# Two overlapped batches: a loop of passes with barriers, or one sequence of 256 head slots

## The reference

```
x = x + tanh(g_xattn[0]) * L0_xattn(layernorm(x), ctx)   # CoPE attention
x = x + tanh(g_ffn[0])   * L0_ffn(layernorm(x))          # 8 experts (top 2) and a shared one
x = x + tanh(g_xattn[1]) * L1_xattn(layernorm(x), ctx)   # plain cross attention
x = x + tanh(g_ffn[1])   * L1_ffn(layernorm(x))          # self attention, gated by head
```

```
pos = minimum(flip(cumsum(flip(sigmoid(logits)))), 63)
cope = logits_int[ceil(pos)] * w + logits_int[floor(pos)] * (1 - w),  w = pos - floor(pos)
scores = softmax(logits + cope);  out = scores @ V
```

## Time and profile before

| | |
|---|---|
| median of three runs | 5707.96 us |
| profiled execution, its own time | 5699.91 us |
| span of that execution | 5698.2 us |
| instructions | 64460 |
| VectorE, TensorE, ScalarE, GpSimd busy | 73%, 59%, 40%, 25% |
| bytes moved | 41.52 MB |

### The profile page before, as it was taken

How to read it: one execution, slowest core, us unless ns; L and a number is a source line. 1 busy time by engine, 2 the same in 40 slices (tenths; PEclk the granted TensorE clock), 3 DMA queues, 4 the chain that set the end, 5 groups by cost and what they waited for, 6 DMA issues and landing times. The chain is left out here.

```text
span 5698.2 us, 64460 instructions
## 1 busy us (share of the span) xinstructions
PE 3375.8 (59%) x21126; PEld 2228.9 (39%) x21126; DVE 4138.4 (73%) x8874; ACT 2277.8 (40%) x5185; POOL 1398.0 (25%) x1125
## 2 busy tenths in 40 slices
PE   3256575655657566565665656556575665756576
PEld 2133352433435334352443534334352443524353
DVE  3878597685967858588585967859588585977853
ACT  2434344343434434344343443434344343443432
POOL 0322223131222312223131321312223131231310
PEclk7567686777768677686776867667786776868776
DMA  3000000000000000000000000000000000000000
GB/s 115 0 8 1 10 1 1 10 1 10 1 8 3 1 10 1 10 1 1 10 1 10 1 1 10 1 10 1 10 1 1 10 1 10 1 1 10 1 6 2
DMA packets 42741, 41.52 MB, mean 7 GB/s; under 512 B 6468, under 2 KB 42342, under 8 KB 42360
## 3 DMA queue, kind: packets, MB, share of 16 engines
q1 hardware_dynamic: 33144, 28.46, 1.7%
q10 hardware_dynamic: 9216, 8.39, 0.5%
HBM read 32.64 MB, written 4.19 MB: 6 GB/s over the span
## 5 line engine op out<-in xcount | busy, mean ns | idle before, releaser
L663 PE MATMUL banks<-xn,w 128*128 128x256 f16 x6912 | 958.4, 305 | 220.1 <-ACT h L734 220.1
L585 DVE COPY_PREDICATED banks<-masks,banks 128x448 f32<-128x448 int16 (+5 forms) x1536 | 1031.2, 671 | 74.9 <-PE banks L381 14.0
L514 POOL TENSOR_TENSOR steps<-slope,rises 128x512 f32<-128x512 f32 x256 | 295.3, 1154 | 2686.3 <-DVE masks L577 2384.5
L663 PEld LDWEIGHTS banks<-xn,w 128*128 128x128 f16 x6912 | 740.8, 109 | 419.3 <-ACT h L734 245.5
L470 ACT ACTIVATE core_prob<-z,negmax 128x256 f32<-128x256 f32 x512 | 255.9, 503 | 570.0 <-DVE negmax L609 569.4
L554 DVE TENSOR_TENSOR_SCAN c<-gate,cap 128x514 f32<-128x514 f32 x256 | 323.6, 1264 | 183.3 <-ACT gate L446 183.3
L521 POOL TENSOR_TENSOR neg_rest<-shift,c 128x512 f32<-128x512 bf16 x256 | 298.3, 1165 | 464.0 <-DVE masks L577 423.3
L676 PE MATMUL banks<-w,a 128*128 128x256 f32 x1152 | 313.6, 421 | 104.2 <-DVE o L838 66.4
L525 POOL TENSOR_TENSOR partial<-partial,core_scores 128x512 f32<-128x512 f32 x256 | 365.9, 1429 | 1.2
L603 DVE TENSOR_TENSOR_SCAN z<-keep,steps 128x512 f32<-128x512 bf16 x256 | 328.8, 1284 | 40.7 <-issue 38.7
L577 DVE TENSOR_SCALAR masks<-shift 128x512 int16<-128x512 int16 x1536 | 335.4, 290 | 7.8
(11 more groups left out here) (254 smaller groups left out, 6846.6 us busy)
## 6 DMA issues: line engine op xcount, KB each, us to landing
stage<-in_L_ffn_w SPq DMA_DIRECT2D x16, 512.0 KB, 5.1
z<-in_ctx ACTq DMA_DIRECT2D x32, 128.0 KB, 2.7
core_pT<-in_x ACTq DMA_DIRECT2D x32, 128.0 KB, 3.0
u<-in_ctx SPq DMA_DIRECT2D x32, 128.0 KB
x<-in_x SPq DMA_DIRECT2D x32, 128.0 KB
out<-x SPq DMA_DIRECT2D x32, 128.0 KB, 1.7
stage<-in_L_ffn_w SPq DMA_DIRECT2D x8, 256.0 KB, 7.1
stage<-in_L_ffn_sw SPq DMA_DIRECT2D x2, 512.0 KB, 4.4
```

The lines of the kernel that those rows point to most:

```text
L514: nc.gpsimd.tensor_tensor(k.steps[:], k.slope[:], k.rises[:, h % 2], ALU.mult).then_inc(sem["core_steps"], 1)
L585: move = nc.vector.copy_predicated(tab[:, :, 0:S - b], k.masks[:, n, :, 0:S - b], tab[:, :, b:S])
L663: last = nc.tensor.matmul(k.bank[bank][:, f * S:(f + 1) * S], w[:, e, a, c, par, f * P:(f + 1) * P], k.x_parts[:, b, c, :], start=(n == 0) ...
```

## The change

The passes and the loop go. `all_batches` replaces `run_pass`: each engine gets one straight program of 275 slots (SLOTS = 256 + 16 + 3). Head g = 16 b + h runs in slot g. Semaphores are never cleared; each wait adds what the batches before have raised (`raised_by`, PER_BATCH). The side pieces of batch b begin in slot 16 (b+1) + 3 (LAG) and are spread over 16 slots. The same rule as before gives the counts 4,3,4,3,4,3,4,3,20,12,4,3,4,21,11,3 (positions 0 to 15).

The core's projections become generators too (`ahead_tensor`, `ahead_scalar`, `ahead_pool`, `ahead_vector`) of 15 pieces: 0 transposed context, 1 norm, 2 transposed x, 3 keys, 4 queries, 5 offset, 6 to 13 the eight stacks, 14 values. All of them use bank 2. Batch 0's run before the slots; those of batch b+1 run from slot 4 of batch b, one per slot at the slot's end (AHEAD: two in slot 4, the 14th in slot 16, the last in slot 19). Other edits: ScalarE does gates and kept scores before the exp, and all its side pieces after both; TensorE does raw scores before the second part of the pieces; transposed probabilities and weighed values share bank 3; `z` is gone, the second scan works in place in `steps`, which gets two buffers; `core_scores` gets a third; `core_offset` and `core_sums` get one per parity of the batch; the core's projections get buffers of their own (`ahead`), and four of the six `pT` buffers lie on xn, xT, ctxT and o. The first three side pieces change order and banks. SP issues all loads and stores: the core's loads of batch b+1 early, the side's context when the gated heads of batch b-1 have been read, and x of a batch after the store of the batch before has landed.

The core of the diff:

```
-    for s in range(H + 3):
-        if s < H:
+    for s in range(SLOTS):
+        pieces, first = side_pieces(s)
+        if s < G:
             act.wait_ge(sem["core_shift"], s + 1)
 ...
-        h = s - 2
-        if 0 <= h < H:
-            act.wait_ge(sem["core_z_ready"], NT * (h + 1))
 ...
-        for _ in range(FIRST[s]):
-            next(side, None)
-        if s + 1 < H:
+        if s + 1 < G:
             gates(s + 1)
             keep_scores(s + 1)
+        g = s - 2
+        if 0 <= g < G:
+            act.wait_ge(sem["core_z_ready"], NT * (g + 1))
 ...
+        for _ in range(first):
+            next(side)
 ...
             nc.scalar.activation(whole(k.slope), k.bank[1][:], ACT.Copy).then_inc(sem["core_slope"], 1)
+        for _ in range(ahead_pieces(s)):
+            next(ahead, None)
```

```
+def side_pieces(s):
+    return (PIECES[(s - LAG) % H], FIRST[(s - LAG) % H]) if s >= H + LAG else (0, 0)
+def ahead_pieces(s):
+    return AHEAD[s % H] if s >= 4 and s < G + 4 else 0
+def raised_by(b):
+    return {name: b * n for name, n in PER_BATCH.items()}
```

```
+def ahead_tensor(nc, k, pe, b):
 ...
+    pe.wait_ge(sem["core_xT_ready"], at["core_xT_ready"] + 1)
+    feature_projection(nc, k.wk_cope, k.core_ctxT, bank).then_inc(sem["core_k_psum"], 1)
+    yield
+    pe.wait_ge(sem["core_k_second"], at["core_k_second"] + NC)
+    feature_projection(nc, k.wq_cope, k.core_norm.xT, bank).then_inc(sem["core_q_psum"], 1)
+    yield
 ...
+    for m in range(P // HB):
+        if m >= 1:
+            pe.wait_ge(sem["core_q_stack"], at["core_q_stack"] + m)
+        stack_pair(nc, k, 1, k.core_k_parts, m, bank).then_inc(sem["core_k_stack_psum"], 1)
+        yield
+        pe.wait_ge(sem["core_k_stack"], at["core_k_stack"] + m + 1)
+        stack_pair(nc, k, 0, k.core_q_parts, m, bank).then_inc(sem["core_q_stack_psum"], 1)
+        yield
```

```
+            for b in range(B):
+                if b >= 1:
+                    if b + 1 < B:
+                        core_loads(b + 1)
+                    sp.wait_ge(sem["gated_heads_psum"], NT * b)
+                for t in range(NT):
+                    sp.dma_start(k.ctx[:, t, :], k.ctx_rows(b, t)).then_inc(sem["loads"], 16)
+                if b >= 1:
+                    store(b - 1)
+                for t in range(NT):
+                    sp.dma_start(k.norm.x[:, t, :], k.x_rows(b, t)).then_inc(sem["loads"], 16)
 ...
-        run_pass(nc, k, 0, None)
-        with nc.Fori(1, B) as i:
-            run_pass(nc, k, i, i - 1)
-        run_pass(nc, k, None, B - 1)
+        zero(nc, k)
+        all_batches(nc, k)
```

More of the change, by code:

```diff
@@ L442, in gates, with core_scalar @@
+    yield
+def core_scalar(nc, k, act, side, ahead):
+    sem = k.sem
+    def gates(g):
+        act.wait_ge(sem["core_scores"], g + 1)
+        if g >= 1:
+            act.wait_ge(sem["core_shift"], g)
+            act.wait_ge(sem["core_gates"], g)
         gate = k.gate[:, :, 0:S]
@@ L493, in core_scalar @@
+        for _ in range(pieces - first):
+            next(side)
+        if s < G:
             act.wait_ge(sem["core_moved"], s + 1)
@@ L1182, in _ @@
+            store(B - 1)
         @block.gpsimd
         def _(pool):
-            side = side_pool(nc, k, pool) if rest is not None else iter(())
-            if core is not None:
-                core_pool(nc, k, pool, side)
-            for _ in side:
-                pass
+            side = chain.from_iterable(side_pool(nc, k, pool, b) for b in range(B))
+            ahead = chain.from_iterable(ahead_pool(nc, k, pool, b) for b in range(B))
+            for _ in range(sum(AHEAD)):
+                next(ahead)
@@ L1190, in _ @@
+            core_pool(nc, k, pool, side, ahead)
         @block.tensor
         def _(pe):
-            side = side_tensor(nc, k, pe) if rest is not None else iter(())
-            if core is not None:
-                core_tensor(nc, k, pe, side)
-            for _ in side:
-                pass
+            side = chain.from_iterable(side_tensor(nc, k, pe, b) for b in range(B))
+            ahead = chain.from_iterable(ahead_tensor(nc, k, pe, b) for b in range(B))
+            for _ in range(sum(AHEAD)):
+                next(ahead)
@@ L1207, in _ @@
[L1207 to L1208 removed]
+            side = chain.from_iterable(side_scalar(nc, k, act, b) for b in range(B))
+            ahead = chain.from_iterable(ahead_scalar(nc, k, act, b) for b in range(B))
+            for _ in range(sum(AHEAD)):
+                next(ahead)
+            core_scalar(nc, k, act, side, ahead)
         @block.vector
         def _(dve):
[L1212 to L1215 removed]
@@ L1216, in _ @@
-            for _ in side:
-                pass
-            if core is not None:
-                core_tail(nc, k, dve, step)
+            side_step = stepper(dve, sem["dve_side"])
+            core_step = stepper(dve, sem["dve_core"])
+            side = chain.from_iterable(side_vector(nc, k, dve, side_step, b) for b in range(B))
+            ahead = chain.from_iterable(ahead_vector(nc, k, dve, core_step, b) for b in range(B))
+            for _ in range(sum(AHEAD)):
+                next(ahead)
```

692 lines of the change are left out of this document (375 added, 317 removed).

## The result

| | before | after |
|---|---|---|
| median of four runs, same chip | 5706.52 us | 5472.07 us (5467.52 to 5474.97) |
| ratio, 95% interval | | 0.959 (0.957 to 0.961) |
| profiled execution, its own time and span | 5699.91, 5698.2 | 5467.52, 5465.6 |
| instructions | 64460 | 63933 |

The change makes the kernel 4.1% faster. The forecast was 5209 us, range 4950 to 5440: the direction was right, the time lies 263 us above the forecast and 32 above the range.

A forecast was written before the change was run, and what follows sets the result against it. Bound: VectorE in the slots, latency in the seams. To slot 18 384.9, plus 14 x 307.7 and 249 mixed, 44.6, 212.8 for the last batch, 1.7 around the span, 8.05 to the median: 5209 us, range 4950 to 5440.

The forecast's parts named there:

- T: Time of sixteen mixed slots, one steady batch carrying core and side work: 307.7 us against 345.5 before.
- VectorE's work: VectorE's busy time per steady batch, claimed unchanged: 237.1 in the slots plus 18.3 in the seam, 255.4 us.
- gates wait, taken out of the idle: Scan's wait for ScalarE's gates inside slots: 7.7 us a batch would go, as gates are issued earlier.
- scoresT pieces from the seam: Gated attention pieces moved from seam into dense slots: 6.3 us of idle a batch, between 0 and 14.8.
- y wait, logits: Cope output projection and gated end: waits of 5.6 and 2.8, together 8.4 us a batch, at best 0.
- projections ahead: Next batch's projections, one piece at each slot's end: 7.0 us of VectorE waits a batch, bounds 0 and 15.
- the rest of the idle time: VectorE's idle inside slots, 38.3 us a batch, less the 7.7 behind gates: 30.6 left.
- (d): Boundary wait, perhaps x's store and reload, still drains engines: 7 to 15 us a batch, 5310 to 5430; chance 0.05.
- (a): Core and side work mix in slots with no moved stall showing: steady batch 286.0, time 4888 us; chance 0.16.
- Rival (c): Next batch's projection pieces hold up the core chain: slower than before, steady batch over 341.4 us; chance 0.05.
- Rival (b): Lumpy slots 8 and 13, all 14.8 us of scoresT exposed: steady batch 324.2, time 5453 us; chance 0.19.
- the port turns: VectorE's two-input operations taking turns with GpSimd once seam work stands in slots: about 2 to 3 us dearer a batch.

The follow-up runs named there:

- e4: Changed kernel with the projections of batches 1 to 15 left out, so every batch uses batch 0's: 113 us less than the changed kernel.
- e3: Changed kernel with ScalarE's old order restored, exp and first side pieces ahead of gates and kept scores: 56 us slower than the changed kernel.
- e10: Changed kernel without products, exps and weighings of both side attentions (the scoresT pieces): 479 us less than the changed kernel.
- e1: Changed kernel with slope's copy and the next table ahead of the slot's last four pieces at positions 9 and 14: no gain.
- e7: Changed kernel with ScalarE's first pieces run in three parts in slots of seven pieces or more: 11 us slower than the changed kernel.
- e5: Changed kernel with 15 of 16 matmuls of every weighing in the side's attentions left out: 22 us less than the changed kernel.
- e12: Changed kernel with slope and table early, assumed piece durations 0.8 for scores and 2.4 for scoresT: 71 us better than with 0.5 and 2.0.
- e9: Changed kernel with scoresT duration 2.0 instead of 1.2 and slope and table early: 97 us slower than with the 2.0 alone.
- e2: Changed kernel with assumed scoresT duration 2.0 instead of 1.2, spreading the same pieces over more slots: same time as the changed kernel.

## Why the prediction was wrong

The miss by its steps, in us: the start up to slot 18 -7.1 (377.8 against 384.9), the mixed stretch +274.4 (from there to 5209.0, against 4556.8), slots 256 to 258 +2.4, the last batch -3.2, profiled execution against median -3.5. Together 263.0. All of it is T: 326.2 in the batch shown (327.2 on average) for 307.7, 18.5 x 14.8 = 274.

T by its terms, in us:
```
term                               predicted  measured
VectorE's work                       255.4     252.9
gates wait, taken out of the idle      0        10.0  as table wait, positions 8 and 9
scoresT pieces from the seam           6.3      14.9  as table wait, positions 13 and 14
y wait, logits                         8.4       7.6  (4.8 + 2.8)
projections ahead                      7.0       3.2
the rest of the idle time             30.6      37.6
sum                                  307.7     326.2
```
**Right.** VectorE's work stayed, the seam went, and x's store and reload held nothing up (neither VectorE nor TensorE nor ScalarE waits for that load), so (d) is out. (a) is out by T. The scan waits for gates once, 1.2 us, where it had waited 183.3 in all. The y wait was 5.6 by forecast and 4.8 by the row, the gated end 2.8 and 2.8. The start was 167.2 for 174.8. Rival (c) is out: e4 gives the whole price of the pieces ahead as 7.4 us a batch against 11.6 (7.0 and 4.6 of work); k and q first parts, forecast 1.4 and 2.3 late, don't wait at all, only v (2.3) and rstd (0.9) do.

**The step that failed** is "Of this the 7.7 us behind the gates go". I took a wait off VectorE at the one place where it stood and didn't ask what VectorE waits for next. Next is the table of the next head; the table waits for the slope, and ScalarE copies the slope behind all side pieces of the slot, in the old order as in the new. Gates and kept scores moved up, the end of ScalarE's chain stayed where it was, and VectorE came earlier to a longer wait. In the cross attention, where the earlier trace rows had 6.7 of its 7.7 us of gates wait (from 1571 to 1613), the table wait is 10.0. e3 shows the exchange on the chip: 287 us of one for 224 of the other, and in the two slots of scoresT nothing at all was gained. The net worth of the new order is 63 us of idle, about 4 a batch, not 7.7. A second thing that the step left out is that the old order would have cost more in the new program: there (e3) the gates wait is 19.4 us a batch, not 7.7. That this comes of sixteen slots holding what nineteen held is likely, but no run tests it apart.

**The mis-sized term** is the scoresT one, 6.3 of a bound of 14.8; the measured 14.9 is the upper bound. I took the idle time of an 11-piece slot over as it stood, 6.0 us. But that slot of 18.5 us held 12.5 us of VectorE's work, the last maxima among it. The slot at position 14, with eleven pieces too, holds 8.7 us of it and takes 20.8: 12.1 idle. Of the 6.1 more than in my row, 3.8 come of less work and 2.3 of a longer slot. The length comes with the new order: e3 has this slot at 18.4 us in thirteen of fourteen batches, with 8.5 us of work. (My reading of the seam was off too, without weight in the sum: three of the sixteen scoresT pieces ran on ScalarE before 1671 and thirteen after, not fifteen.) With the 10.0 of the cross attention the 14.9 is one thing: two dense slots a batch, each with a chain of ScalarE, TensorE and ScalarE. e10 takes the pieces out and 29.5 us of a steady batch go, the table wait with them. e1 shows that it is a chain and not a place in the order. I had both bounds and the sentence that "table(s+1) stands behind them on TensorE, slope(s) on ScalarE"; the rows above follow it through one slot: eleven pieces and one copy take ScalarE from 3280.5 to 3295.2, while VectorE has work until 3285.6.

**Rival (b)** has T right, 324.2 for 326.2, and time, 5453 for 5472, for a partly wrong reason. All 14.8 of the scoresT are exposed, as it said. Its 2.5 us each for slots 8 and 13 answer to table waits of 2.1 and 4.0 behind them, though the slots took 21.1 and 21.3 us, under the 25 that I had named as its sign; the larger waits, 7.9 and 10.9, stand behind 9 and 14. And the port turns, 3 us dearer by its count, became no dearer. Of the signs that I had named, the last one is what happened: the masked copies waited for the table by over 10 us a batch. That "the piece order is what failed" was half right: e1 and e7 alone, both orders, give nothing.

**Rest.** The remaining idle grew by 7.0. Of this 5.5 is the wait for the weighed values (L1229) after the slot at position 9 (the other 1.6 of that row is in the gated end of the table). It is the same chain seen from its other end, as e1's exchange shows.

What stays open: how the chain divides between ScalarE's own core work, TensorE's and the hops between the two (e5 hardly changed TensorE's time, e10 takes all three away). That TensorE's clock has a share in it is shown by the last section. Open too is where e12's weights take 144 us of e9's idle time from.

## What to carry over

When a wait is to be removed by moving instructions up, ask what the waiting engine needs next, and whether that stands at the end of the same chain: if it does, the wait only changes its name. Value a dense slot by the longest chain through it and not by the wait that the profile names. When the idle time of a slot is taken over as an estimate, take its length over and set the new slot's own work against it. And read busy time beside idle time: two versions of equal time (the changed kernel and e2) can be one step from very different ones.

## What the runs showed of the hardware

**The pace of VectorE's two-input passes hangs on GpSimd's timing, by 84 us for two lines in the whole kernel.** One form in the changed kernel, then in e2 (busy us, mean ns | idle before):
```profile
L946 DVE SCALAR_TENSOR_TENSOR a<-xT,eg_eth 128x512 f32<-128x512 f32 x144 | 142.0, 986 | 5.0
```
```profile
L946 DVE SCALAR_TENSOR_TENSOR a<-xT,eg_eth 128x512 f32<-128x512 f32 x144 | 99.6, 692 | 5.0
```
L943 goes the same way, 975 to 684 ns. Single ones of the changed kernel take 0.69 us with GpSimd idle and 1.64 beside it:
```profile
3048.52 0.69 DVE L946 SCALAR_TENSOR_TENSOR a<-xT,eg_eth 128x512 f32<-128x512 f32 x1
...
3061.92 1.64 DVE L946 SCALAR_TENSOR_TENSOR a<-xT,eg_eth 128x512 f32<-128x512 f32 x1
...
3061.30 1.71 POOL L618 TENSOR_TENSOR partial<-partial,core_scores 128x512 f32<-128x512 f32 x1
```
In the changed kernel, as in the one before, 45 of each line's 144 passes run beside a GpSimd instruction (mean 1.62 and 1.63 us) and 99 with GpSimd idle (0.68 and 0.69). In e2 all 144 find it idle: the counts happen to put them there. The two lines make 84 us, and three other two-input passes (L1193 to L1196) 41 more; L247 takes 13 less, the scan L660 16 more, and the whole is 118 less. The Trainium skill (SBUF — State Buffer, Who interferes with whom) says that a VectorE instruction with two SBUF inputs contends with a GpSimd instruction that reads SBUF; these rows agree, GpSimd's L618 being stretched too, 1.27 to 1.71 us. I had used the rule for a price of the moved work; its worth was in the expert slots, which did not move between the batches.

**Fewer matmuls came with a lower granted clock of TensorE.** In e5 the slot at position 14 has 64 matmuls at 0.50 for 106 at 0.58, and TensorE is busy 12.9 us for 14.0. 1792 matmuls less in the kernel leave its busy time at 3423.8 for 3431.0; its mean granted clock is 0.693 for 0.712.

**A dense slot's length follows TensorE's granted clock, by over 1.5 us.** In the changed kernel the slot at position 9 has the same 104 matmuls in all fourteen batches. In four the granted clock is 0.78, TensorE is busy 10.5 to 10.7 us and the slot takes 18.1; in ten it is 0.67, TensorE is busy 12.2 to 12.3 and the slot takes 19.6 to 20.2. The batch shown in the section on the result is one of the four. In e3 the slot at position 14 takes 18.4 us in thirteen batches at 0.69 and 20.4 in the one at 0.50, with the same 106 matmuls.
